# Queries and keys from split values, expert weights in nine pieces, 32 tiles routed early, maxima four pairs later

## The reference

```python
qkv = x @ W_qkv.T + b_qkv                                  # q, k, v of 8 features for 16 heads
att = einsum('bthd,bshd->bhts', q, k) / sqrt(8)
x1  = layernorm(x + (softmax(att) @ v) @ W_out.T + b_out)
s   = sigmoid(x1 @ gate_w.T)                               # 8 experts
sel = top_k(s + expert_bias, 2)                            # first index wins a tie
h_e = silu((x1 * s_e) @ w1[e].T) * ((x1 * s_e) @ w3[e].T)  # for both chosen experts
y   = shared(x1) + sum_e s_e * (h_e @ w2[e].T)
out = layernorm(x1 + y)
```

## Time and profile before

| what | value |
|---|---|
| median of three runs | 780.76 us (778.63 to 780.85) |
| the profiled execution, whole | 777.83 us |
| its span | 776.0 us |
| PE busy | 749.5 us (97%) |
| DVE busy | 643.2 us (83%) |
| ACT busy | 512.9 us (66%) |
| POOL busy | 476.5 us (61%) |

### The profile page before, as it was taken

The page is one execution under the profiler, slowest core; times in us unless marked ns, Lnnn a source line. Parts: engine busy times, 40 slices in busy tenths (PEclk is TensorE's granted clock), DMA queues, the critical chain, the costliest instruction groups (busy, mean ns, idle before and its releaser), DMA issues.

```text
span 776.0 us, 20315 instructions
## 1 busy us (share of the span) xinstructions
PE 749.5 (97%) x6948; PEld 525.7 (68%) x6948; DVE 643.2 (83%) x1389; ACT 512.9 (66%) x1037; POOL 476.5 (61%) x653
## 2 busy tenths in 40 slices
PE   4899999999999999999997999999999999999996
PEld 2255555555555555555553688888888888888886
DVE  7789999999999999999997656878676666667676
ACT  2178888988888888888887745555554545544542
POOL 5445778776676767667534366566565566555564
PEclk9999999999999999999999999999999999999999
DMA  4757875657566565655520554645454545555650
GB/s 115 185 141 179 221 196 153 187 147 183 156 156 170 145 191 150 170 163 150 153 71 22 165 136 115 128 124 134 131 128 127 129 129 127 128 120 123 125 114 27
DMA packets 201470, 108.90 MB, mean 140 GB/s; under 512 B 10408, under 2 KB 201000, under 8 KB 201384
## 3 DMA queue, kind: packets, MB, share of 16 engines
q1 hardware_dynamic: 199792, 105.75, 53.1%
q10 hardware_dynamic: 1592, 2.05, 1.1%
HBM read 73.41 MB, written 33.82 MB: 138 GB/s over the span
## 4 chain that ended last, share of the span: by engine, by line
PE 93%; DVE 3%; DMA 1%; issue 1%; ACT 0%; SPq 0%; POOL 0%; POOLq 0%; DVEq 0%; ACTq 0%
PE bank L907 16%; PE bank L732 16%; PE bank L704 11%; PE bank L739 9%; PE bank L740 9%; PE bank L741 9%; PE bank L717 8%; PE bank L809 3%; PE bank L789 2%; PE bank L829 2%; PE bank L796 2%; PE bank L813 2%; PE bank L861 1%; PE bank L836 1%; DVE negmax L1058 1%
## 5 line engine op out<-in xcount | busy, mean ns | idle before, releaser
L578 ACT ACTIVATE probs<-bank 128x512 f32<-128x512 f32 x512 | 291.8, 606 | 61.9 <-PE bank L704 57.6
L1058 DVE TENSOR_REDUCE negmax<-bank 128x2 f32<-128x512 f32 x512 | 319.8, 679 | 11.3 <-PE bank L717 8.8
L678 ACT ACTIVATE q_stack<-k_stack 128x512 f32<-128x512 f32 x128 | 80.8, 631 | 151.2 <-DVE k_stack L1121 151.1
L717 PE MATMUL bank<-k_stack,q_stack 48*128 48x256 bf16 x1024 | 164.1, 281 | 3.2 <-DVE negmax L1058 1.8
L704 PE MATMUL bank<-q_stack,k_stack 50*128 50x256 bf16 x1024 | 157.4, 275 | 1.1 <-ACT probs L578 0.7
L1121 DVE TENSOR_TENSOR k_stack<-bank,probs 128x512 f32<-128x512 f32 x128 | 88.3, 690 | 73.8 <-PE bank L741 69.6
L732 PE MATMUL bank<-probs,v_aug 128*32 128x256 f32 x2048 | 137.6, 386 | 0.4 <-ACT attT L589 0.4
L704 PEld LDWEIGHTS bank<-q_stack,k_stack 50*128 50x128 bf16 x1024 | 75.7, 95 | 84.5 <-ACT probs L578 43.3
L739 PE MATMUL bank<-x_hi,hi_w 128*128 128x512 f32 x288 | 126.4, 439 | 0.8 <-DVE res L1070 0.5
L740 PE MATMUL bank<-x_hi,lo_w 128*128 128x512 f32 x288 | 114.0, 396 | 0.0
L741 PE MATMUL bank<-x_lo,hi_w 128*128 128x512 f32 x288 | 113.6, 394 | 0.0
(11 more groups left out here) (110 smaller groups left out, 1142.9 us busy)
## 6 DMA issues: line engine op xcount, KB each, us to landing
probs<-route_dram SPq DMA_DIRECT2D x128, 256.0 KB, 4.9
q_stack<-q_parts_dram SPq DMA_DIRECT2D x64, 192.0 KB, 3.2
k_stack<-k_parts_dram SPq DMA_DIRECT2D x64, 192.0 KB, 4.0
k_parts_dram<-k_parts SPq DMA_DIRECT2D x32, 192.0 KB, 2.2
q_parts_dram<-q_parts SPq DMA_DIRECT2D x32, 192.0 KB, 2.2
xT_sb<-xT SPq DMA_DIRECT2D x32, 128.0 KB, 2.2
k_parts_dram<-k_parts SPq DMA_DIRECT2D x32, 128.0 KB, 2.0
q_parts_dram<-q_parts SPq DMA_DIRECT2D x32, 128.0 KB, 2.1
```

The costliest lines, as they stand in the source:

```text
L578: nc.scalar.activation(probs[h][:], score_ps[bank(b, h)][:].rearrange("p (j t) -> p j t", j=NT), ACT.Exp).then_inc(exp_done, 1)
L678: nc.scalar.activation(act[n % DEPTH], gated[n % DEPTH] if n else up1_ps[0][:], ACT.Silu).then_inc(act_set, 1)
L717: mm = pe.matmul(max_ps[bank(b, h)][:, i * T:(i + 1) * T], q_stack[b.ring][first:last, h // 2, i * P:(i + 1) * P], k_stack[b.ring][first:l ...
L1058: nc.vector.tensor_reduce(negmax[b.ring % 2][:, :, column], max_ps[bank(b, head)][:].rearrange("p (i s) -> p i s", i=NT), AX_X, ALU.max, n ...
```

## The change

1. **Products from parts.** ACT rounds both weights and the transposed x to fp32r (`wk_hi`, `wq_hi`, `xT_hi`), POOL subtracts to get the rest (`wk_lo`, `wq_lo`, `xT_lo`). From batch 4 on, each key and query product is three fp32r matmuls over 256 columns, not one float32 product. xT_hi is made at step 10 of the turn before, xT_lo at the end of POOL's turn.
2. **The norm's `var_eps`** (128x2) moves from DVE to POOL, in front of `rstd`.
3. **`MAX_FROM` is 8, not 6.** The switch of batch comes one pair later.
4. **Expert weights** come in nine DMAs of three experts, one a turn in turns 2 to 10 at ACT's step 4, not three DMAs in turns 2 to 4 at step 12.
5. **Routing.** 32 tiles are routed early, not 48, at other steps: scores after the transposes of turn 30 (step 10, not 5), the rest in turn 31; PE's transposes at pair 7, not 6. 32 tiles are routed late, not 16, with the reciprocal in two halves.

```diff
-        def expert_slot(m):
-            return 2 + m
+        def expert_slot(m, n):
+            return 2 + m * (NE // 3) + n // 3
+        FROM_PARTS = 4
+        def parts(b, more=0):
+            return b.c - FROM_PARTS + (1 + more)
-        MAX_FROM = 6
+        MAX_FROM = 8
-        EARLY = (CHUNKS - 1) * CHUNK
-        DVE_SCORES, DVE_FIRST, DVE_SECOND, DVE_WEIGHTS, DVE_ROUTED = (-2, 5), (-2, 10), (-1, 5), (-1, 6), (-1, 13)
-        ACT_ROUTE, ACT_SPLIT, PE_ROUTED = 4, 15, 6
+        EARLY_CHUNKS = 2
+        EARLY = EARLY_CHUNKS * CHUNK
+        DVE_SCORES, DVE_FIRST, DVE_SECOND, DVE_WEIGHTS, DVE_ROUTED = (-2, 10), (-2, 11), (-1, 5), (-1, 10), (-1, 14)
+        ACT_LOAD, ACT_ROUTE, ACT_SPLIT, PE_ROUTED = 4, 4, 15, 7
...
+                    pool.wait_ge(mv_set, b.count(NT, NT))
+                    pool.tensor_scalar(var_eps[:], mv[:, :, 1], EPS, None, ALU.add).then_inc(eps_set, 1)
...
+                if t.soft.c == -2:
+                    for n, (low, whole, high) in enumerate(((wk_lo, wk_sb, wk_hi), (wq_lo, wq_sb, wq_hi))):
+                        pool.wait_ge(wqk_hi_set, n + 1)
+                        pool.tensor_tensor(low[:], whole[:], high[:], ALU.subtract).then_inc(wqk_lo_set, 1)
+                b = t.load
+                if b.live and b.c >= FROM_PARTS:
+                    pool.wait_ge(xT_hi_set, parts(b))
+                    pool.tensor_tensor(xT_lo[:], xT_sb[b.ring][:], xT_hi[:], ALU.subtract).then_inc(xT_lo_set, 1)
...
+                    a = t.load
+                    if a.live and h == ACT_HI and a.c >= FROM_PARTS:
+                        act_e.wait_ge(xT_in[a.ring], a.lap(16, 16))
+                        act_e.wait_ge(q_mm, a.count(1, 0))
+                        nc.scalar.activation(xT_hi[:], xT_sb[a.ring][:], ACT.Copy).then_inc(xT_hi_set, 1)
...
+                    if t.proj.live and h == ACT_LOAD:
                         for m in range(3):
-                            if t.soft.c == expert_slot(m):
-                                load_expert(m)
+                            for n in range(0, NE, 3):
+                                if t.soft.c == expert_slot(m, n):
+                                    load_expert(m, n)
...
+            def from_parts(ps, hi, lo):
+                pe.matmul(ps, hi[:], xT_hi[:], start=True, stop=False)
+                pe.matmul(ps, lo[:], xT_hi[:], start=False, stop=False)
+                return pe.matmul(ps, hi[:], xT_lo[:], start=False, stop=True)
...
-                        pe.matmul(right, wk_sb[:], xT_sb[b.ring][:], start=True, stop=True).then_inc(k_mm, 1)
+                        if b.c < FROM_PARTS:
...
+                            pe.wait_ge(xT_lo_set, parts(b))
+                            from_parts(right, wk_hi, wk_lo).then_inc(k_mm, 1)
...
+                    elif b.live and p == PE_VQ:
+                        from_parts(right, wq_hi, wq_lo).then_inc(q_mm, 1)
...
-                        nc.vector.tensor_scalar(var_eps[:], mv[:, :, 1], EPS, None, ALU.add).then_inc(eps_set, 1)
...
                 if (g, n) == (LATE_FIRST, 3):
-                    sigmoid(a, b)
+                    plus_one(a, b)
+                if (g, n) == (LATE_FIRST, 4):
+                    inverse(a, (a + b) // 2)
                 if (g, n) == (LATE_FIRST, 5):
+                    inverse((a + b) // 2, b)
+                if (g, n) == (LATE_FIRST, 6):
                     with_bias(a, b)
```

More of the change, by code:

```diff
@@ L96, in attention_moe_layer @@
         minus_half, ones = sb("minus_half", [P, GT]), sb("ones", [P, NT, 2, PAIRS])
+        wq_hi, wq_lo, wk_hi, wk_lo = (sb(n, [P, C], F32R) for n in ("wq_hi", "wq_lo", "wk_hi", "wk_lo"))
+        xT_hi, xT_lo = sb("xT_hi", [P, T], F32R), sb("xT_lo", [P, T], F32R)
         x1T = sb("x1T", [P, N])
@@ L354, in slot @@
                 if t.soft.c == B - 1:
-                    route_to_dram(slice(0, CHUNKS - 1), 1)
+                    route_to_dram(slice(0, EARLY_CHUNKS), 1)
                 if b.live:
@@ L880, in _ @@
             pe.wait_ge(w_lo_set, 2 * NE // 3)
-            pe.wait_ge(expert_in[2], 16)
+            for piece in expert_in[2]:
+                pe.wait_ge(piece, 16)
             pe.wait_ge(exp_done, H * B)
@@ L992, in first_of_ranked, with plus_one, inverse, sigmoid @@
                 route(nc.vector.tensor_tensor(sel[:, tiles], equal[:, tiles], best[:, tiles].unsqueeze(2).to_broadcast(full), ALU.is_equal))
[L994 removed]
+            def plus_one(a, b):
                 tiles = slice(a, b)
                 route(nc.vector.tensor_scalar(scores[:, tiles], scores[:, tiles], 1.0, None, ALU.add))
+            def inverse(a, b):
+                tiles = slice(a, b)
                 route(nc.vector.reciprocal(scores[:, tiles], scores[:, tiles]))
+            def sigmoid(a, b):
+                plus_one(a, b)
+                inverse(a, b)
             def with_bias(a, b):
@@ L1035, in slot @@
                     if (t.soft.c - B, h) == DVE_ROUTED:
-                        routing_to_sbuf(max_ps[2], 0, CHUNKS - 1, 1)
-                    if not t.soft.looped and (t.soft.c - B, h) == DVE_SCORES:
+                        routing_to_sbuf(max_ps[2], 0, EARLY_CHUNKS, 1)
+                    turn = (t.soft.c - B, h)
+                    if turn == DVE_SCORES:
                         dve.wait_ge(c_in, 16 * 5)
@@ L1040, in slot @@
                         dve.wait_ge(score_mm, H * (B - 2))
-                        biased_scores(0, EARLY)
-                    if not t.soft.looped and (t.soft.c - B, h) == DVE_FIRST:
-                        first_choice(0, EARLY)
-                    if not t.soft.looped and (t.soft.c - B, h) == DVE_SECOND:
-                        second_choice(0, EARLY)
-                    if not t.soft.looped and (t.soft.c - B, h) == DVE_WEIGHTS:
+                        sigmoid(0, EARLY)
+                        with_bias(0, EARLY)
+                    if turn == DVE_FIRST:
+                        highest(0, EARLY)
+                        by_rank(0, EARLY)
+                    if turn == DVE_SECOND:
+                        first_of_ranked(0, EARLY, first_sel)
+                        without_first(0, EARLY)
+                        highest(0, EARLY)
+                        by_rank(0, EARLY)
+                    if turn == DVE_WEIGHTS:
+                        first_of_ranked(0, EARLY, equal)
                         weights_of_both(0, EARLY)
+                        assert step[0] == ROUTE_STEPS[0]
                     if t.norm.live and h == DVE_STATS:
@@ L1186, in late_routing @@
                     weights_of_both(a, b)
+                    assert step[0] == ROUTE_STEPS[1]
             def group(g, r):
```

53 lines of the change are left out of this document (22 added, 31 removed).

## The result

| | before | after |
|---|---|---|
| median of five runs | 780.18 us (778.63 to 780.85) | 772.97 us (771.91 to 773.29) |
| profiled execution | 777.83 us | 773.07 us |
| its span | 776.0 us | 771.3 us |

The ratio is 0.9914, with a 95% interval of 0.9895 to 0.9933. The forecast was 774.8 us in a range of 770.5 to 780.5, and faster: it holds, at a gain of 0.9% whose interval is clear of no change. But it was made from a profile, where 6.0 us were to go and 4.8 went.

The account below looks back on a forecast made before the run. PE was taken to bound turns 0 to 27, DVE turns 28 and 29. 3.9 + 0.2 + 1.0 + 1.5 - 0.2 = 6.4, less 0.4, gave 6.0 us: 780.8 - 6.0 = 774.8 us, range 770.5 to 780.5.

Parts of the forecast that it names:

- Products: Key and query products, batches 4 to 31: three fp32r matmuls take 0.36 us, not 0.43; 3.9 us gained (2.8 to 6.2).
- first rival: Products from parts: weight loads set the pace, three matmuls take 0.70 us; 793.8 us, or about 804; chance 0.06.
- var_eps: Turns 28 and 29: DVE loses this step, 0.2 us gained; on POOL it takes 0.25 us plus 0.05 handover.
- second rival: POOL is late in each turn: var_eps costs 0.72 us, PE's transposes wait about 0.2 us; 780.4 us; chance 0.13.
- Ramp: Turns before turn 0: 24 maxima stand ahead, not 26; 1.0 us gained, ends 0 and 1.3.
- Turn 30: Maxima go before routing there, so PE's transposes of the maxima start sooner; 2.0 us gained, before the give-back.
- Give-back: Turn 31 to the experts' first weighing: weights arrive late, 0.5 of turn 30's 2.0 us lost again, leaving 1.5.
- Late routing: Groups 2 to 4: 17 late operations on twice the tiles, some 3 us of DVE; 0.2 us lost, ends 0 and 1.0.
- fourth rival: Groups 2 and 3: late routing holds up PE by contention, 2 to 3 us; 777.5 us; chance 0.08.
- Small waits: PE waiting on POOL and ACT in 28 tighter turns; 0.4 us lost.
- nine weight pieces: DMAs issued from ACT's queue, one a turn in nine turns: cost nothing, at worst 0.1 us.
- Rivals 3 and 4: Rival 3: ramp and turn 30 give nothing, only products gain, 3.5 us, 777.3 us; chance 0.15. Rival 4: the fourth rival.

Follow-up runs that it names:

- Maxima from step 6: The changed kernel with the switch of batch at step 6 again (MAX_FROM 6, not 8); median 772.97 us, profiled 772.82 us.
- late routing spread: Changed kernel, late routing's bias at round 8 of group 2, each choice in rounds 2 to 4 of groups 3 and 4; median 773.27 us.
- old routing: Changed kernel with 48 tiles routed early at their old places, 16 late, maxima still from step 8; median 776.28 us, profiled 778.41 us.
- var_eps thrice: Changed kernel with the addition of the small constant to the variance done three times on POOL; median 781.65 us, profiled 782.36 us.

## Why the prediction held, and which terms were off

- **Products, 3.9 us: right in mechanism, a little too small.** 0.078 us each instead of 0.07. The 3.90 us of the table are 25 of the 28 turns; all 56 products would make 4.4 us, an estimate by the same price. The pace goes by columns: 0.117 us for 256, half of the 0.234 for 512. The first rival is out, since no load shows in it. By the rule of the Trainium skill ("TensorE: Matmul & The Clock Gate", section "Part 3: Packing small matmuls — row/col tiling"), a load would have overlapped only from another row group; the trace disagrees for this shape as well. The same section also lets a load go ahead of matmuls in flight when it targets the background weight buffer, and with that the trace agrees.
- **var_eps, 0.2 us: 0.04.** POOL's price is 0.23 us, as bounded by L488. The second rival had the right mechanism: with 0.61 us more ahead of it `max_two` makes PE wait, and the room was 0.31 us, as against my 0.3.
- **Ramp, 1.0 us: not seen in the two profiles.** Turn 0's scores came 0.97 us sooner. By turn 3 the lead was 0.46 us, and the six products of turns 0 to 2 are 0.47 of that by the price above. PE left half pace 1.6 us later in this execution than in that of before (below), which hides the ramp's part. Maxima from step 6 put its size at 0.73 us, but there too the change of pace came 0.7 us later, so this is within the scatter of the start.
- **Turn 30, gain of 2.0 us: 2.65, and 0.5 more in turn 31.** I had the transposes at 6.1 to 6.2 us after `res`. They came at 409.34 - 403.81 = 5.5. I also had the routing end at 11.3 us and the next `res` at 12.6, "hidden". The routing ended at 11.87, and `res` followed at 11.90.
- **Give-back of 0.5 us: 1.78. This term failed.** The step was "DVE's copy comes 0.7 us later in turn 31; fewer bytes give back perhaps 0.2". The copy comes 8.0 us after `res` (423.70 - 415.71) instead of 7.1, so 0.9 later. The experts' round 0 starts 10.9 us after `res` instead of 11.4, so 0.5 sooner, and waits that much more. And from the start of the copy to the first weighing it took 7.72 us instead of 7.28, so 0.4 more: copy and write got shorter with fewer bytes, but the read took 0.8 us longer. I had counted the first of these alone, and for the third a gain of 0.2.
- **Late routing, 0.2 us: 1.0, its end.** "PE does not wait for DVE there" failed: it waited 0.46 us at round 28. The 3 us more of DVE are spread over 60 us only on average; where they stand behind the statistics and the norm of a group, DVE has no gap to take them. The fourth rival had this, at two to three times the size.
- **Small waits, 0.4 us:** none. The turn is 12.14 us, which is 12.30 less the two products.

The nine weight pieces, "nothing", are borne out in turns 3 to 27. Of the signs, PE's wait in turn 30, the turn, the products, `var_eps` and turn 0's scores came as said; the wait for `probs` grew by 2.05 us, not by 0.5, and PE was not unbroken in groups 2 to 5.

The sum on the profile was 1.2 us too large. I then carried it over to the median unchanged, and the medians moved by 2.4 us more than the profiles. The two misses went opposite ways, and it is luck that 774.8 us came within 1.8 us of the result. Rivals 3 and 4 were each partly true: what turns 30 and 31 gained less what the expert stage gave back was 3.18 - 1.78 - 1.00 = 0.4 us in the profiles.

## What to carry to other kernels

A stall of TensorE can cost more than its own length, where its clock then stays low (3.4 to 6.8 us at 0.50 behind stalls of 2.85 to 3.67 us here), and the second part varies from execution to execution; look at the granted clock behind each long wait, and at the mean clocks of all runs before you carry a profile's difference over to a median. When a stall ahead of a transfer goes, everything up to the transfer's consumer gets shorter and the transfer doesn't: place its start anew. Cheap work moved into "idle time" must be placed against the rounds in which the engine has none.

## What the runs showed that I had not expected

- In the ramp PE leaves half pace at a moment that varies. 16 matmuls of PE in the kernel after (first fence) and in that with the late routing spread, whose program is the same there:

```profile
44.71 1.94 PE L762 MATMUL bank<-probs,v_aug 128*32 128x256 f32 x16
48.32 1.07 PE L762 MATMUL bank<-probs,v_aug 128*32 128x256 f32 x16
```

```profile
44.26 1.07 PE L762 MATMUL bank<-probs,v_aug 128*32 128x256 f32 x16
```

  Both profiles give 1.00 as the granted clock from 44 to 48 us, but that column has nothing to go by there: the trace's record of the clock begins at 47.38 us in the first and at 43.76 us in the second, and the time ahead of it is counted as full. In all 14 profiles the slow matmuls lie ahead of the moment at which the record begins, 43.76 to 49.00 us, and the full pace behind it. 1.94 us is what these matmuls took at a granted 0.50 in the old routing, so I read the stretch ahead as the lower level. The `res` of turn 3 came between 75.43 and 76.83 us in eight executions of kernels alike up to there but for var_eps in one, and in the order of that moment: 43.76 us with 75.43, 45.31 with 76.06 (twice), 45.89 with 76.20, 46.26 with 76.55, 46.79 with 76.75, 47.38 with 76.77, 47.79 with 76.83. So the scatter of the start is this moment. Why it varies is open. A single pair of profiles cannot judge an effect in the ramp below 1.4 us, unless this moment is set beside it.
- The same DVE operation with two SBUF inputs took 0.42 and 1.38 us (L1027), 0.45 and 1.34 us (L1022), in one execution. A POOL operation with two SBUF inputs was under way when each of the long ones started (POOL from 414.12 to 415.39 and from 491.77 to 493.05 us). In var_eps thrice DVE started L1030, the same step, at 423.01, 0.19 us ahead of POOL's; DVE took 0.50 us, and POOL's took 1.44 instead of 1.27. Beside POOL's `x_new` (418.38 to 420.22), which reads one large tensor, both took the short time.
- From the issue of the weights' read to the first weighing it took 4.58 to 6.47 us. It was 4.58, 4.92 and 6.47 us in the three kernels with the old routing. Why is open; no run tells it.
